# A state space layer: taps as products with a spread column, the sum with one on GpSimd, statistics in three slot pairs, turned steps behind the next inputs

## What is computed

```python
xz = xt @ in_proj                                   # 128 -> 512: x half and gate half
xc, z = xz[..., :256], xz[..., 256:]
xconv = conv_b                                      # causal convolution over time, 4 taps
for kk in range(4):
    xconv = xconv + conv_w[:, kk] * xp[:, kk:kk + T, :]      # xp: xc with 3 zeros ahead
xc = silu(xconv)
dbc = xc @ x_proj
dt = softplus(dbc[..., :8] @ dt_w + dt_b)
Bm, Cm = dbc[..., 8:24], dbc[..., 24:]
dA = exp(dt[..., None] * -exp(A_log))
dBx = (dt * xc)[..., None] * Bm[:, :, None, :]
# scan over time: h = dA_t * h + dBx_t ;  y_t = sum over states of h * C_t
y = (ys + Dp * xc) * silu(z)
return y @ out_w + out_b
```

## Time and profile before

| | |
|---|---|
| median of 3 runs | 4123.09 us (4118.75 to 4128.67) |
| the profiled execution | 4131.86 us, its span 4130.2 us |
| state space stage, first to last scan | 505.9 to 2364.6 us |
| busy share of the whole span | TensorE 78%, VectorE 73%, ScalarE 63%, GpSimd 60% |
| mean granted clock of TensorE | 0.874 |

### The profile page before, as it was taken

One profiled execution on the slowest core, in us unless ns is written; L12 is line 12 of the kernel. 1 busy time (PEld: TensorE's weight loads), 2 busy tenths in 40 slices (PEclk: granted clock), 3 DMA queues, 4 the chain that ended last, 5 costly groups with the idle time before them and its releaser, 6 DMA issues. The chain is left out here.

```text
span 4130.2 us, 82487 instructions
## 1 busy us (share of the span) xinstructions
PE 3215.0 (78%) x29152; PEld 2209.4 (53%) x29152; DVE 3025.6 (73%) x5960; ACT 2602.7 (63%) x5235; POOL 2473.4 (60%) x2815
## 2 busy tenths in 40 slices
PE   7999588887888788878887777678875975668576
PEld 4776255555555555555555546346653643357446
DVE  3999388887888888888878846638985855069754
ACT  5887487787778777877887621026766627148462
POOL 3899378888888888888888300026865412024750
PEclk8999699999999999999999956777767967889788
DMA  3000100000000000000000051240000010700234
GB/s 87 25 25 27 40 11 15 22 22 17 17 22 22 16 17 22 22 15 18 22 19 12 16 134 42 103 177 27 27 1 5 1 23 21 285 8 1 82 83 118
DMA packets 271006, 172.53 MB, mean 42 GB/s; under 512 B 41648, under 2 KB 249976, under 8 KB 268536
## 3 DMA queue, kind: packets, MB, share of 16 engines
q1 hardware_dynamic: 270600, 167.25, 13.8%
HBM read 116.59 MB, written 50.60 MB: 40 GB/s over the span
## 5 line engine op out<-in xcount | busy, mean ns | idle before, releaser
L1212 DVE TENSOR_TENSOR_SCAN mam_hs<-mam_dA,mam_ps_b 128x1024 f32<-128x1024 f32 x512 | 1142.5, 2273 | 164.4 <-PE mam_ps_b L981 157.8
L995 PE MATMUL mam_ps_h<-mam_ident,mam_hs 128*128 128x128 f32 x4096 | 568.1, 283 | 162.8 <-ACT mam_hTb L1140 153.7
L1132 ACT ACTIVATE mam_dA<-mam_dt,mam_A 128x496 f32<-128x496 f32 x1024 | 654.6, 709 | 0.4
L995 PEld LDWEIGHTS mam_ps_h<-mam_ident,mam_hs 128*128 128x128 f32 x4096 | 467.9, 145 | 328.1 <-issue 255.0
L1140 ACT COPY mam_hTb<-mam_ps_h 128x512 f32<-128x512 f32 x768 | 422.5, 585 | 102.0 <-PE mam_ps_h L995 101.3
L981 PE MATMUL mam_ps_b<-mam_DB,mam_dtxt 32*128 32x512 f32 x2048 | 320.1, 695 | 90.4 <-DVE mam_hs L1212 90.4
L1007 PEld LDWEIGHTS mam_ps_y<-mam_hTb,mam_WC 128*32 128x32 f32 x8192 | 217.7, 114 | 215.9 <-issue 111.1
L771 POOL TENSOR_SCALAR mam_tap<-mam_xcp,mam_cw 128x557 f32<-128x557 f32 x180 | 318.9, 1772 | 17.5
L1222 DVE COPY mam_hTb<-mam_ps_h 128x512 f32<-128x512 f32 x256 | 173.4, 677 | 164.3 <-PE mam_ps_h L995 155.2
L1007 PE MATMUL mam_ps_y<-mam_hTb,mam_WC 128*32 128x128 f32 x8192 | 289.8, 284 | 0.3 <-issue 0.3
L772 POOL TENSOR_TENSOR mam_cv<-mam_cv,mam_tap 128x557 f32<-128x557 f32 x180 | 246.3, 1368 | 15.0
(11 more groups left out here) (721 smaller groups left out, 8294.8 us busy)
## 6 DMA issues: line engine op xcount, KB each, us to landing
moe_wg<-in_L_ffn_weight SPq DMA_DIRECT2D x32, 1024.0 KB, 7.9
rnn_xr<-x SPq DMA_DIRECT2D x23, 512.0 KB, 6.3
l1y_wh<-mode_weights SPq DMA_DIRECT2D x16, 544.0 KB, 3.7
gat_hg<-in_x SPq DMA_DIRECT2D x16, 512.0 KB, 7.1
h<-gat_out SPq DMA_DIRECT2D x32, 256.0 KB, 2.3
mam_ht<-h SPq DMA_DIRECT2D x128, 64.0 KB, 2.0
mam_hr<-h SPq DMA_DIRECT2D x128, 64.0 KB, 2.1
mam_xt<-in_x SPq DMA_DIRECT2D x128, 64.0 KB, 2.1
```

Of the source, the lines that this page charges most:

```text
L995: last = pe.transpose(ps_h[n][:, q * P:(q + 1) * P], hs[:, w % 3, c:c + P], ident[:, :])
L1132: act.activation(dA[:, h, :, n, 1:], dt[:, i % 2, h, :].rearrange("p (q t) -> p q t", q=Q)[:, :, 1:], ACT.Exp, scale=A[:, h, n:n + 1]).the ...
L1212: dve.tensor_tensor_scan(hs[:, w % 3, :], dA[:, h, first:first + 2, :, :].rearrange("p q s t -> p (q s t)"), ps_b[:, 2 * (w % 2):2 * (w % ...
```

## The change

Four things, all in `mamba`.

1. **Convolution.** `xcp` becomes a tile of nodes x 35 columns, `cv` and `tap` lose the gaps (512 columns). On GpSimd each product is now a two-input `tensor_tensor` with the weight column spread over all columns. Only the three leading columns of each node are zeroed.
2. **Sum with one.** `one_more` on VectorE goes; `plus` on GpSimd forms it right behind its own sum, and waits for `dt_ready` of the turn before ahead of both.
3. **Output side.** `moments` is split: `statistics` in slot 11, aggregate and variance in slot 13, `scale` in slot 15 (was 13). `deviations` goes from slot 12 to 14, `finish` from slot 14 to slot 11 of the next turn.
4. **Order.** On TensorE `split_c` and `turn_steps` stand behind the next inputs instead of ahead of them. On ScalarE `logarithms` goes from slot 9 to 8, the decays of half 0 start in slot 9 instead of 10, and `c_in` and `turned_steps_in` follow their producers. On GpSimd `plus`, `spread_c` and `time_steps` change places.

```diff
             def convolve(i, h):
-                L = NP - K + 1
...
-                acc = cv[:, h, 0:L]
-                step(pool.tensor_scalar(acc, xcp[:, h, 0:L], cw[:, h, 0:1], None, ALU.mult))
+                acc = nodes(cv[:, h, :])
+
+                def weight(k):
+                    return cw[:, h, k:k + 1].unsqueeze(2).broadcast_to([P, Q, T])
+
+                step(pool.tensor_tensor(acc, xcp[:, h, :, 0:T], weight(0), ALU.mult))
                 for k in range(1, K):
-                    step(pool.tensor_scalar(tap[:, 0:L], xcp[:, h, k:k + L], cw[:, h, k:k + 1], None, ALU.mult))
-                    step(pool.tensor_tensor(acc, acc, tap[:, 0:L], ALU.add))
+                    step(pool.tensor_tensor(tap[:, :, :], xcp[:, h, :, k:k + T], weight(k), ALU.mult))
+                    step(pool.tensor_tensor(acc, acc, tap[:, :, :], ALU.add))
...
             def plus(i, h):
                 pool.wait_ge(dt_read, 2 * i + h + 1)
                 pool.wait_ge(e_ready, 2 * i + h + 1)
+                if i >= 1:
+                    pool.wait_ge(dt_ready, 2 * (i - 1) + h + 1)
...
+                pool.tensor_scalar(ln[:, h, :], e[:, h, :], 1.0, None, ALU.add).then_inc(e1_ready, 1)
...
@@ GpSimd's table
-                if u == 0 and turn(k):
-                    spread_c(k, 2)
+                if u == 0 and turn(k + 1):
+                    plus(k + 1, 1)
                 if u == 1:
                     if turn(k + 2) and k + 2 >= EARLY:
                         convolve(k + 2, 0)
-                    if turn(k + 1):
-                        plus(k + 1, 1)
+                    if turn(k):
+                        spread_c(k, 2)
...
-                if u in (9, 10) and turn(k + 1):
-                    time_steps(k + 1, u - 9)
-                if u == 12 and turn(k - 1):
-                    deviations(k - 1)
-                if u in (13, 15) and turn(k + 1):
-                    spread_c(k + 1, (u - 13) // 2)
-                if u == 14 and turn(k - 1):
-                    finish(k - 1)
-                if u == 15 and turn(k + 2):
-                    plus(k + 2, 0)
+                if u == 9 and turn(k + 1):
+                    time_steps(k + 1, 0)
+                    time_steps(k + 1, 1)
+                if u == 11 and turn(k - 2):
+                    finish(k - 2)
+                if u == 14:
+                    if turn(k + 1):
+                        spread_c(k + 1, 0)
+                    if turn(k - 1):
+                        deviations(k - 1)
+                if u == 15:
+                    if turn(k + 2):
+                        plus(k + 2, 0)
+                    if turn(k + 1):
+                        spread_c(k + 1, 1)
@@ TensorE's table: ahead of sums and flip in the slot
+                if u == 12 and turn(k + 1):
+                    split_c(k + 1)
+                if u == 14 and turn(k + 1):
+                    turn_steps(k + 1, 0)
+                if u == 0 and turn(k):
+                    turn_steps(k, 1)
...
-                if u in (13, 15) and turn(k + 1):
-                    turn_steps(k + 1, (u - 13) // 2)
@@ ScalarE's table
-            first1, first0 = (0, 3, 6, 9, 12, 16), (0, 2, 6, 9, 11, 14, 16)
+            first1, first0 = (0, 3, 6, 9, 12, 16), (0, 2, 4, 7, 9, 11, 14, 16)
...
-                if u == 9 and turn(k + 1):
+                if u == 8 and turn(k + 1):
                     logarithms(k + 1)
...
@@ VectorE's table
-                if u == 5 and turn(k + 1):
-                    lost(k + 1, 0)
-                    one_more(k + 1, 1)
-                if u == 7 and turn(k + 1):
-                    lost(k + 1, 1)
+                if u in (5, 7) and turn(k + 1):
+                    lost(k + 1, (u - 5) // 2)
...
-                    moments(k - 1)
+                    statistics(k - 1)
+                if u == 13 and turn(k - 1):
+                    moments(k - 1)
-                if u == 13 and turn(k - 1):
+                if u == 15 and turn(k - 1):
                     scale(k - 1)
-                if u == 15 and turn(k + 2):
-                    one_more(k + 2, 0)
```

More of the change, by code:

```diff
@@ L623, in mamba @@
     V = U // 2
-    NP = Q * PADT
     S4 = S // 4
@@ L642, in mamba @@
         hT = s.sb("hT", [P, N])
-        xcp = s.sb("xcp", [P, HV, NP])
-        cv, tap = s.sb("cv", [P, HV, NP]), s.sb("tap", [P, NP])
+        xcp = s.sb("xcp", [P, HV, Q, PADT])
+        cv, tap = s.sb("cv", [P, HV, N]), s.sb("tap", [P, Q, T])
         xs, sz = s.sb("xs", [P, 3, HV, N]), s.sb("sz", [P, 3, HV, N])
@@ L751, in _ @@
             step(pool.memset(half_c[:, :], -0.5))
-            step(pool.memset(xcp[:, :, :], 0.0))
+            step(pool.memset(xcp[:, :, :, 0:K - 1], 0.0))
             step(pool.memset(dA[:, :, :, :, 0:1], 0.0))
@@ L1029, in _ @@
                     project_bc(k + 2)
-                if u == 11 and turn(k + 1):
-                    split_c(k + 1)
                 if u in (12, 14) and turn(k + 2):
                     time_steps(k + 2, (u - 12) // 2)
-                if u in (13, 15) and turn(k + 1):
-                    turn_steps(k + 1, (u - 13) // 2)
                 if u % 2 == 1 and pair((w + 1) // 2):
@@ L1064, in x_in @@
                     act.wait_ge(conv_first, 2 * (i - 1) + h + 1)
-                act.copy(nodes(xcp[:, h, :])[:, :, K - 1:], nodes(ps_0[:, :])).then_inc(xc_ready, 1)
+                act.copy(xcp[:, h, :, K - 1:], ps_0[:, :].rearrange("p (q t) -> p q t", q=Q)).then_inc(xc_ready, 1)
             def silu_x(i, h):
@@ L1073, in silu_x @@
                     act.wait_ge(y_taken, 2 * (i - 3) + h + 1)
-                act.activation(nodes(xs[:, i % 3, h, :]), nodes(cv[:, h, :])[:, :, 0:T], ACT.Silu, bias=cb[:, h:h + 1]
-                               ).then_inc(xs_ready, 1)
+                act.activation(xs[:, i % 3, h, :], cv[:, h, :], ACT.Silu, bias=cb[:, h:h + 1]).then_inc(xs_ready, 1)
             def silu_z(i, h):
@@ L1168, in _ @@
                     states_of_input(k + 2)
+                if u == 12 and turn(k + 1):
+                    c_in(k + 1)
                 if u in (13, 15) and turn(k + 2):
                     softplus(k + 2, (u - 13) // 2)
+                if u == 14 and turn(k + 1):
+                    turned_steps_in(k + 1, 0)
                 if unit(w - 1):
@@ L1176, in _ @@
                     x_in(k + 2, u // 2)
-                if u == 11 and turn(k + 1):
-                    c_in(k + 1)
-                if u == 13 and turn(k + 1):
-                    turned_steps_in(k + 1, 0)
                 if u < 5 and turn(k):
                     decays(k, 1, first1[u], first1[u + 1] - first1[u])
-                if 10 <= u and turn(k + 1):
-                    decays(k + 1, 0, first0[u - 10], first0[u - 9] - first0[u - 10])
+                if 9 <= u and turn(k + 1):
+                    decays(k + 1, 0, first0[u - 9], first0[u - 8] - first0[u - 9])
         @block.vector
@@ L1197, in convolve @@
                     dve.wait_ge(xs_ready, 2 * (i - 1) + h + 1)
-                x, acc = nodes(xcp[:, h, :]), nodes(cv[:, h, :])[:, :, 0:T]
-                step(TS(acc, x[:, :, 0:T], cw[:, h, 0:1], None, ALU.mult))
+                acc = nodes(cv[:, h, :])
+                step(TS(acc, xcp[:, h, :, 0:T], cw[:, h, 0:1], None, ALU.mult))
                 for k in range(1, K):
-                    step(STT(out=acc, in0=x[:, :, k:k + T], scalar=cw[:, h, k:k + 1], in1=acc, op0=ALU.mult,
+                    step(STT(out=acc, in0=xcp[:, h, :, k:k + T], scalar=cw[:, h, k:k + 1], in1=acc, op0=ALU.mult,
                              op1=ALU.add))
@@ L1223, in states_in @@
                                 ps_h[1][:, :].rearrange("p (q d) -> p q d", q=S4)).then_inc(hB_ready, 1)
-            def one_more(i, h):
-                n = 2 * i + h
-                dve.wait_ge(e_ready, n + 1)
-                if i >= 1:
-                    dve.wait_ge(dt_ready, n - 1)
-                TS(ln[:, h, :], e[:, h, :], 1.0, None, ALU.add).then_inc(e1_ready, 1)
             def lost(i, h):
@@ L1250, in residual, with statistics @@
                    ).then_inc(z_ready, 1)
-            def moments(i):
+            def statistics(i):
                 dve.wait_ge(z_ready, i + 1)
@@ L1255, in moments @@
                     step.mark(dve.bn_stats(st[:, g, :], z[:, g, :]))
+            def moments(i):
                 step.join()
```

## The result

The changed kernel takes 3870.43 us (median of 4 runs, 3864.02 to 3883.1), the kernel before 4125.88 us (median of 4, 4118.75 to 4132.69). The ratio is 0.9381, 95% interval 0.9365 to 0.9397: faster by 255 us, where 229 were forecast. The profiled execution took 3872.9 us (span 3871.1).

The account below looks back on a forecast made before the run. Waits between engines bound the kernel: links of 24.9 and 26.4 us make a 51.3 us turn against 59.1, saving 226 us over 29 turns, 229 with edges. Forecast 3903 us profiled, 3894 median; range 3845 to 3995.

Parts of the forecast that it names:

- What bounds the kernel: State space layer: no engine is full; waits between engines set the 59.10 us turn, as two links in series.
- link A: Scan 0 to ScalarE's second SiLU of the x half, set by GpSimd's convolutions: 31.0 us, forecast 24.1 to 25.0.
- The convolution: On GpSimd: two-input products of 512 columns at 1.05 us each; a convolution takes 8.6 us, 3.1 saved per half.
- The sum with one: Moved from VectorE to GpSimd as a one-input instruction, two a turn, 1.6 us each (bounds 1.27 and 1.77).
- Link B: ScalarE's queue from the second SiLU to the last decay: 28.8 us, forecast 26.4.
- Priced alone they are worth nothing beyond this: Split statistics and moved turned steps and C split: 6.0 us of waits removed from the last three pairs, beside link B.
- The lock: VectorE's four scalings beside busy GpSimd, sharing a port: 1.6 us more a turn, 0.2 us on the path.
- the rival: Shared port and GpSimd take part back: scalings, variance sum and losses wait; turn 54.3 us, 3981 us; chance 0.21.
- better still: ScalarE's and GpSimd's waits vanish; turn nears 49.8 us, kernel 3850 us; chance 0.11.

Follow-up runs that it names:

- run 2: Changed kernel with the old convolution put back (one-input products of 557 columns): 4102.72 us, ratio 0.9929.
- run 8: Changed kernel with one extra subtraction (1.35 us) on GpSimd each turn, directly ahead of the second convolution: 3920.88 us, ratio 0.9492.
- run 3: Changed kernel with the sum with one back on VectorE: 3896.56 us, ratio 0.9431.
- run 4: Changed kernel with the statistics as before (moments in slot 11, scaling in 13, `deviations` in 12, `finish` in 14): 3938.77 us, ratio 0.9535.
- run 5: Changed kernel with the C split and turned steps ahead of TensorE's inputs again, their ScalarE copies at the old places: 3923.13 us, ratio 0.9508.
- run 9: Changed kernel with half 0's decays redistributed, moving one from behind slot 14's flips into the wait for slot 12's: 3867.03 us, ratio 0.9368.
- run 6: Changed kernel with two further copies of 512 columns, 0.6 us each, on ScalarE in each turn: 3883.00 us, ratio 0.9401.
- run 7: Changed kernel with two extra subtractions (2.7 us) on GpSimd each turn, just ahead of `finish` in slot 11: 3882.98 us, ratio 0.9398.
- run 10: Changed kernel with one of ScalarE's flip-bank copies a turn (slot 14, second bank) given to VectorE: 3880.08 us, ratio 0.9401.
- run 11: Changed kernel with the edits of run 9 and run 10, and ScalarE's first gate SiLU behind the copy of slot 5: 3875.53 us, ratio 0.9388.
- run 12: Kernel of run 11 with one more unused GpSimd product a turn, shifting the short C spreads under VectorE's scalings: 3898.14 us, ratio 0.9448.

## Why the prediction was right, and where it was not

The forecast was a turn of 51.3 us; it is 50.40. For the profiled execution 3903 was forecast and 3872.9 measured: of these 30 us the turns are 29 x 0.9 = 26, and the edges, which gave 7 us instead of 3, the other 4. Against the medians (3894 and 3870.4) the error is 24 us, because this profiled execution lies 2.5 us above its median and not 8.8.

- **What bounds the kernel**: right. GpSimd's second convolution set link A; with it gone ScalarE's wait went from 193.8 to 1.4 us. Undoing it brings the stall back (run 2), and work put ahead of it costs its own length (run 8).
- **The convolution**: product 1.05 us as taken, by the exact likeness in the earlier trace rows. The Trainium skill (GPSIMD Engine Reference, section 3.1) has a two-input instruction at some 2.6 cycles per element. At that page's 1.2 GHz 512 columns are an estimated 1.11 us; the 1.27 that the prediction put down to the page is the measured price of L790. The 1054 ns of 180 instructions lie 5% below that estimate and do not contradict it. What the rows contradict is that an instruction with one input is the cheaper: the sum with one, of the same width, takes 1494 ns. The sum in the convolution is 1.33 us instead of 1.27; one of 1.60 overlaps a `lost` on VectorE (1333.55 above), and that such meetings make the whole difference is not shown. The second convolution is 8.83 us (1331.29 to 1340.12), taken as 8.6.
- **The sum with one**: 1.49 us, taken as 1.6. Moving it is worth some 21 to 26 us (run 3).
- **Link A**: 23.8 us (1316.30 to 1340.12), taken as 24.9; this is the term that was mis-sized. The first product begins 2.33 us after scan 0 and not 3.15, an effect that the prediction saw (up to 0.9) and did not take. From there to the second convolution it is 12.66 us instead of 13.2, and the convolution 0.2 more. ScalarE was to wait 1 to 2 us at this SiLU and waits in 2 turns of 29: GpSimd comes 1.1 us sooner than forecast, and ScalarE 0.7 later (about 23.9 us after scan 0, taken as 24.45 less 1.3).
- **Link B**: 50.4 - 23.8 = 26.6 us, taken as 26.4. The size is right, the place of its remaining idle time is not: about 1.0 us was to come back mostly at the first decay, which was to wait for GpSimd's step sizes. ScalarE waits there not at all; its 1.5 us of link B lie at flip copies (0.32, 0.95 and 0.18 us).
- **"Priced alone they are worth nothing beyond this"**, of the statistics in three pairs and the moved steps: this step failed as an account of the parts, not in the sum. Undone one at a time they cost 64 us (0.9535 against 0.9381, run 4) and 52 us (run 5). Neither lies beside link B for free. The runs show the place of both, and it is link A: without the first, GpSimd's two round trips to VectorE stand ahead of the convolution in its queue; without the second, the x input comes 0.8 us later. The prediction had seen the x copy's part ("up to 0.9 sooner") and left it out of its sum; GpSimd's round trips it had not looked at.
- **The lock**: the prediction let the four scalings grow to 2.9 us with 0.2 on the path. In the changed kernel they take 1.19, beside the four short spreads of C and a gap, with nothing on the path. That they stayed short was luck of the placing: 0.5 us of shift makes them 2.5 (run 9). It shows instead at `lost`, which only the rival had looked at: 942 ns in the mean before, 1348 ns now, 0.8 us a turn of VectorE's time, in the pairs of slots 4 and 6. The store hardly ever holds the scalings up (2.4 us of waiting in 128 instructions).
- **The rival "better still"** had its argument half right: ScalarE's wait for the convolution and GpSimd's for the scalings did vanish, and the turn came 0.6 us from its 49.8. GpSimd still waits 47.8 us for the variance and 35.5 for the x input.

What ends the turn now is not one engine. Added work reaches the turn in part on ScalarE (run 6), whole ahead of the convolution (run 8), hardly behind it (run 7). Relief for ScalarE comes back as longer scalings on VectorE and as waits, mostly for flips in run 10 and for GpSimd in run 11. Whether relief at VectorE's end alone would reach the turn is not shown, since run 12 also gave GpSimd 1 us more. No variant beat the changed kernel beyond the intervals.

## What to carry to other kernels

Where one wait stands above all others, price the parts of a change in the order in which they come free: here the same edits were worth 28 us ahead of the convolution's repair and 97 us behind it. Where several engines arrive within a few tenths of a microsecond of each other, as after this change, relief for one of them was absorbed by the next (runs 9 to 11); that less work on all, or a shorter round trip, would move the turn is my guess, which no run tested. Look, too, at where a forecast gain or loss lands and not only at its size: run 5 gave the expected time from another place. And before moving a short VectorE instruction, look at how long the GpSimd instruction beside it is.
